# First tiles of a token-mixing and expert kernel: statistics and scans reordered, one transposed copy split in two

## The reference

```python
x0 = layernorm(x)                                 # no gain, no shift
xn1 = layernorm(x0) * g1 + b1
r, w, k, v = sigmoid(xn1 @ Wr.T), -exp(xn1 @ Ww.T), xn1 @ Wk.T, xn1 @ Wv.T
e = exp(w + k)
num[s], den[s] = decay*num[s-1] + e*v, decay*den[s-1] + e      # along the 512 tokens
tm = (r * num / (den + 1e-8)) @ Wo.T
a = x0 + tm
xn2 = layernorm(a) * g2 + b2
a = a + sigmoid(xn2 @ Wrec.T) * (square(relu(xn2 @ Wkey.T)) @ Wval.T)   # 512 hidden
x = x + a
h = layernorm(x)
x = x + shared_expert(h) + top1_of_16_experts(h)
```

## Time and profile before

| | us |
|---|---|
| median of 3 runs | 489.94 (489.55 to 490.75) |
| the profiled execution | 489.72 |
| its span | 487.7 |
| PE busy in the span | 475.4 (97%) |
| DVE busy | 370.0 (76%) |
| POOL busy | 352.1 (72%) |
| ACT busy | 323.9 (66%) |

### The profile page before, as it was taken

How to read it: one execution, slowest core, us unless ns; L and a number is a source line. 1 busy time by engine, 2 the same in 40 slices (tenths; PEclk the granted TensorE clock), 3 DMA queues, 4 the chain that set the end, 5 groups by cost and what they waited for, 6 DMA issues and landing times.

```text
span 487.7 us, 10435 instructions
## 1 busy us (share of the span) xinstructions
PE 475.4 (97%) x3079; PEld 386.6 (79%) x3079; DVE 370.0 (76%) x1056; ACT 323.9 (66%) x623; POOL 352.1 (72%) x573
## 2 busy tenths in 40 slices
PE   8998999999999999999999999999999999999995
PEld 7654777868777778686777867888899999999995
DVE  7889899899999999996899989837445555545535
ACT  2766887988978879777687886554265565555521
POOL 6665688898888988986788777777336676667760
PEclk9999999999999999999999999999999999999998
DMA  7007001101101011010101101110389755442018
GB/s 237 1 2 280 24 21 45 56 13 65 34 32 66 24 45 54 12 65 23 46 23 44 41 4 45 45 43 34 114 195 264 200 153 149 134 132 82 30 50 296
DMA packets 33031, 39.33 MB, mean 81 GB/s; under 512 B 4913, under 2 KB 29113, under 8 KB 32720
## 3 DMA queue, kind: packets, MB, share of 16 engines
q1 hardware_dynamic: 26640, 24.98, 17.7%
q0 software_dynamic: 5760, 13.16, 7.8%
q10 hardware_dynamic: 576, 0.52, 0.3%
HBM read 21.69 MB, written 17.93 MB: 81 GB/s over the span
## 4 chain that ended last, share of the span: by engine, by line
PE 83%; POOL 4%; DVE 4%; issue 4%; ACT 2%; DMA 1%; SPq 0%; POOLq 0%; DVEq 0%; ACTq 0%
PE bank L427 20%; PE bank L420 10%; PE bank L444 6%; PE bank L435 5%; PE bank L414 4%; PE bank L835 4%; PE bank L836 4%; PE bank L828 4%; PE bank L528 3%; PE bank L540 2%; PE bank L519 2%; PE bank L524 2%; PE bank L514 2%; PE bank L588 2%; PE bank L707 2%
## 5 line engine op out<-in xcount | busy, mean ns | idle before, releaser
L427 PE MATMUL bank<-hT,wm 128*128 128x256 f32 x512 | 124.7, 383 | 0.6 <-ACT kr L942 0.6
L427 PEld LDWEIGHTS bank<-hT,wm 128*128 128x128 f32 x512 | 92.0, 190 | 18.7 <-issue 8.3
L1562 POOL DMA_INDIRECT sorted_rows<-rows,posi x64 | 72.0, 1125 | 19.6 <-issue 16.9
L1646 POOL DMA_INDIRECT out<-shared x55 | 53.2, 967 | 37.3 <-DVE shared L1476 22.2
L420 PEld LDWEIGHTS bank<-wm,k 128*128 128x128 f32 x512 | 61.5, 192 | 7.3 <-issue 5.9
L420 PE MATMUL bank<-wm,k 128*128 128x128 f32 x512 | 62.2, 275 | 0.0
L1118 ACT ACTIVATE er<-bank 128x256 f32<-128x256 f32 x40 | 15.4, 384 | 44.8 <-PE bank L836 44.1
L1484 DVE TENSOR_TENSOR e<-er,bank 128x256 f32<-128x256 f32 x40 | 16.9, 421 | 23.0 <-ACT er L1118 21.1
L444 PE MATMUL bank<-wm,actA 128*128 128x128 f32 x240 | 32.9, 280 | 0.0
L1646 POOL DMA_INDIRECT out<-rows x24 | 23.1, 964 | 11.3 <-DVE rows L1476 5.3
L978 ACT ACTIVATE h<-rows,smE 128x128 f32<-128x128 f32 x64 | 26.3, 482 | 7.1 <-POOL smE L1538 7.1
(11 more groups left out here) (256 smaller groups left out, 1288.4 us busy)
## 6 DMA issues: line engine op xcount, KB each, us to landing
shared<-sorted_rows SPq DMA_DIRECT2D x56, 128.5 KB, 3.1
shared<-x SPq DMA_DIRECT2D x16, 256.0 KB
rows<-sorted_rows SPq DMA_DIRECT2D x24, 128.5 KB
wexp<-w_exp SPq DMA_DIRECT2D x2, 1536.0 KB, 8.3
sorted_rows<-filler SPq DMA_DIRECT2D x17, 128.5 KB
shared<-out SPq DMA_DIRECT2D x6, 256.0 KB, 4.9
out<-shared SPq DMA_DIRECT2D x12, 128.0 KB, 3.1
sorted_rows<-rows,posi POOLq DMA_INDIRECT x64, 2.8
```

Source lines behind the costliest of these rows:

```text
L427: ins = mm(dst[:, j * HALF:(j + 1) * HALF], W(name, 2 * pair_ + j), src[:, half * HALF:(half + 1) * HALF], start=True, stop=True)
L1562: g_.indirect_dma_start(sorted_ap, bass.IndirectOffsetOnAxis(posi[t % 3][:, g:g + 1].bitcast(U32), 0), rows[t % 3][:, g, :], None).then_in ...
L1646: g_.indirect_dma_start(out, bass.IndirectOffsetOnAxis(xr[k % RING][:, j, D:D + 1].bitcast(U32), 0), xr[k % RING][:, j, D + 1:ROW], None, ...
```

## The change

It concerns the first tiles, mostly t < 2 (`IN_HALVES`) and t < 4 (`EARLY_STATS`):

- Load of x(3) is issued ahead of the second part of the weights. DVE's start: decay constant first, statistics of x(2) and x(3) before the first round, two other constants moved into rounds (behind z of tile 0 and of tile 3).
- The scan den of tiles 1 and 2 stands in front of an of the tile before.
- For t < 2 the addition of `rstd` moves from POOL to DVE, and `xa` on POOL stands behind the power of the next tile's `smC`.
- The four products of num and q: POOL in the order 1, 3, 0, and for t < 2 the one of piece 2 on DVE. PE multiplies with Wo in the order 1, 3, 0, 2.
- T2 of tiles 0 and 1 is transposed into two banks (7 and the small bank 1), copied in halves, and the first key is formed in halves.
- T1 of tile 2 moves up in front of R of tile 1, without its warm-up of five products; ACT's copy of it and the exp of R move with it.

```diff
             load_x(2)
+            load_x(3)
             sp.dma_start(wm[:, cut:cut2], w_main[:, cut:cut2]).then_inc(s["w_in1"], 16)
-            load_x(3)
...
+        def T2_of(t, half):
+            return SMALL if t < IN_HALVES and half else T2_B
...
             def keys(t):
-                wait(pe, "xn2T", t)
+                wait(pe, "xn2T", t, 1 if t < IN_HALVES else 2)
...
+                if t < IN_HALVES:
+                    mm(KE_BANK[0][:, 0:HALF], W("Wkey", 0), xn2T[t % 2][:, 0:HALF], start=True, stop=True)
+                    wait(pe, "xn2T", t)
+                    mm(KE_BANK[0][:, HALF:T], W("Wkey", 0), xn2T[t % 2][:, HALF:T], start=True, stop=True).then_inc(s["K0"], 1)
...
                 for t in at(1):
+                    if t == 1:
+                        turn_x(t + 1)
                     if t not in (2, 3):
                         r_product(t)
...
-                        turn_x(t + 2)
-                        warm(WARM_BEFORE[1])
                         w_product(t + 2)
                         r_product(t + 2)
-                    wait(pe, "an", t)
                     wait(pe, "a", t)
-                    transposes(T2_B, an[t % 2], "T2")
+                    for half in range(2):
+                        wait(pe, "an", t, half + 1)
+                        for g in range(2 * half, 2 * half + 2):
+                            ins = nc.tensor.transpose(grp(T2_of(t, half), g), grp(an[t % 2], g), ident[:, :])
+                        ins.then_inc(s["T2"], 1)
...
             def copy_a(t):
+                if t < IN_HALVES:
+                    for half in range(2):
+                        wait(act_e, "T2", t, half + 1)
+                        af(xn2T[t % 2][:, half * HALF:(half + 1) * HALF], T2_of(t, half)[:, half * HALF:(half + 1) * HALF], ACT.Identity,
+                           bias=V("b2"), scale=V("g2")).then_inc(s["xn2T"], 1)
...
                 for t in at(4):
                     copy_a(t)
+                    if t == 0:
+                        exp_r(t + 2)
...
+            def sum_of_e(t):
+                wait(dve, "e", t)
+                wait(dve, "q", t - 2)
+                v.tensor_tensor_scan(den[t % 2][:, :], decay[:, :], e[t % 2][:, :], 0.0, ALU.mult, ALU.add).then_inc(s["den"], 1)
...
+                    if t < IN_HALVES:
+                        wait(dve, "agC", t, 2)
+                        v.tensor_scalar(smC[t % 3][:, 0, :], mvC[t % 3][:, :, 1], 1.0, LN_EPS, ALU.mult, ALU.add).then_inc(s["agC"], 1)
...
-                for t in at(0):
-                    if t == EARLY_STATS:
-                        stats_of_x(t)
+                for t in at(2):
+                    if t in (1, 2):
+                        sum_of_e(t)
                 for t in at(3):
                     norm_a(t)
...
+                    if t < 2:
+                        wait(dve, "num", t)
+                        wait(dve, "rq2", t)
+                        v.tensor_tensor(grp(q[t % 2], 2), grp(num[t % 2], 2), grp(q[t % 2], 2), ALU.mult).then_inc(s["p2"], 1)
...
                 for t in at(5):
-                    sum_a(t)
+                    if t >= 2:
+                        sum_a(t)
                 for t in at(4):
                     wait(gp, "agC", t)
-                    rstd(smC[t % 3], mvC[t % 3], "pC", t)
+                    if t < IN_HALVES:
+                        g_.tensor_tensor(smC[t % 3][:, 1, :], smC[t % 3][:, 0, :], half8[:, 0, :], ALU.pow).then_inc(s["pC"], 2)
+                    else:
+                        rstd(smC[t % 3], mvC[t % 3], "pC", t)
+                for t in at(5):
+                    if t < 2:
+                        sum_a(t)
```

More of the change, by code:

```diff
@@ L69 @@
     den=1, num=1, q=1, rq0=1, p0=1, p1=1, rq2=1, p2=1, TM2=1, p3=1, a=1,
-    agC=2, pC=2, an=1, xa=1, T2=1, xn2T=1, K0=1, kr0=1, k20=1, VAL0=1, K1=1, kr1=1, k21=1, VAL1=1, K2=1,
+    agC=3, pC=2, an=2, xa=1, T2=2, xn2T=2, K0=1, kr0=1, k20=1, VAL0=1, K1=1, kr1=1, k21=1, VAL1=1, K2=1,
     kr2=1, k22=1, VAL2=1, K3=1, kr3=1, k23=1, VAL3=1, REC=1, th=1, rv=1, x2=1, agE=2, pE=3, h=1, T4=1,
@@ L513, in keys @@
                 wait(pe, "ew", t + 1 if t else 2)
-                mm(KE_BANK[0][:, :], W("Wkey", 0), xn2T[t % 2][:, :], start=True, stop=True).then_inc(s["K0"], 1)
+                if t < IN_HALVES:
[3 more added lines that the diff above has]
+                else:
+                    mm(KE_BANK[0][:, :], W("Wkey", 0), xn2T[t % 2][:, :], start=True, stop=True).then_inc(s["K0"], 1)
                 wait(pe, "xn2T", t)
@@ L669, in one_round @@
                     if t == 1:
-                        warm(WARM_BEFORE[0])
+                        warm(WARM_BEFORE)
                     if t != 2:
@@ L713, in one_round @@
                 for t in at(2):
-                    wait(pe, "p0", t)
+                    wait(pe, "p1", t)
                     wait(pe, "xn2T", t - 1)
-                    mm(grp(TM_B, 0), grp(q[t % 2], 0), W("Wo"), start=True, stop=True)
-                    wait(pe, "p1", t)
                     mm(grp(TM_B, 1), grp(q[t % 2], 1), W("Wo"), start=True, stop=True)
@@ L720, in one_round @@
                     mm(grp(TM_B, 3), grp(q[t % 2], 3), W("Wo"), start=True, stop=True)
+                    wait(pe, "p0", t)
+                    mm(grp(TM_B, 0), grp(q[t % 2], 0), W("Wo"), start=True, stop=True)
                 for t in at(5, B_TILES):
@@ L899, in copy_a @@
             def copy_a(t):
-                wait(act_e, "T2", t)
-                af(xn2T[t % 2][:, :], T2_B[:, :], ACT.Identity, bias=V("b2"), scale=V("g2")).then_inc(s["xn2T"], 1)
+                if t < IN_HALVES:
[3 more added lines that the diff above has]
+                           bias=V("b2"), scale=V("g2")).then_inc(s["xn2T"], 1)
+                else:
+                    wait(act_e, "T2", t)
+                    af(xn2T[t % 2][:, :], T2_B[:, :], ACT.Identity, bias=V("b2"), scale=V("g2")).then_inc(s["xn2T"], 2)
             def norm_x(t):
@@ L1045, in one_round @@
                 for t in at(2):
+                    if t == 1:
+                        copy_x(t + 1)
                     if t != 2:
@@ L1146, in bn_stats_of, with bn_aggr_of @@
                 ins.then_inc(s[done], 1)
-            def bn_aggr_of(mv, st, done):
+            def bn_aggr_of(mv, st, done, count=1):
                 for g in range(G):
                     ins = v.bn_aggr(mv[:, g, :], st[:, g, :])
-                ins.then_inc(s[done], 1)
+                ins.then_inc(s[done], count)
             def normed(dst, src, mv, rs, done):
@@ L1155, in normed @@
                     ins = v.tensor_scalar(grp(dst, g), src(g), mv[:, g, 0:1], rs[:, g:g + 1], ALU.subtract, ALU.mult)
-                ins.then_inc(s[done], 1)
+                    if g % 2:
+                        ins.then_inc(s[done], 1)
             def consts():
@@ L1174, in half_tile, with decay_const, rev_const @@
                 const(ins)
-            def more_consts():
+            def decay_const():
+                dve.wait_ge(s["decay_s"], 1)
+                const(v.tensor_scalar(decay[:, :], decay[:, :], decay1[:, 0:1], None, ALU.add))
+            def rev_const():
                 for g in range(G):
@@ L1328, in one_round @@
                     v.tensor_tensor(ew[t % 2][:, :], K_B[:, :], ew[t % 2][:, :], ALU.subtract).then_inc(s["z"], 1)
+                    if t == 0:
+                        rev_const()
+                    if t == 3:
+                        place_const()
                 for t in at(6):
@@ L1360, in one_round @@
                 for t in at(2):
-                    wait(dve, "e", t)
-                    wait(dve, "q", t - 2)
-                    v.tensor_tensor_scan(den[t % 2][:, :], decay[:, :], e[t % 2][:, :], 0.0, ALU.mult, ALU.add).then_inc(s["den"], 1)
+                    if t not in (1, 2):
+                        sum_of_e(t)
                 for t in at(0):
-                    if t > EARLY_STATS:
+                    if t >= EARLY_STATS:
                         stats_of_x(t)
@@ L1408, in _ @@
             half_tile()
+            decay_const()
+            stats_of_x(2)
             consts()
-            more_consts()
-            for t in range(2, EARLY_STATS):
-                stats_of_x(t)
+            stats_of_x(3)
             def last_rounds():
```

20 lines of the change are left out of this document (9 added, 11 removed).

## The result

The changed kernel takes 496.06 us (median of 5 runs, 494.77 to 496.18) against 489.94 (5 runs, not the three named above): ratio 1.0115, 95% interval 1.0104 to 1.0126. One execution of a kernel further down (e6) took 696.52 us at a mean granted clock of 0.657 and is left out of that kernel's ratio. The forecast was 493.2, with 494.9 as the upper end: the direction holds, the size does not. The profiled execution took 496.08 (span 494.4) against 489.72 (487.7).

| event | before | after | later by |
|---|---|---|---|
| statistics of x(4) on DVE | 39.40 | 41.36 | 1.96 |
| a(2) on DVE | 50.52 | 53.72 | 3.20 |
| fourth key of tile 2 on PE | 63.62 | 68.27 | 4.65 |
| T2 of tile 4 on PE, no wait behind it in the steady part | 95.76 | 100.41 | 4.65 |
| last down product of the experts | 466.22 | 470.64 | 4.42 |

What follows compares the result with a forecast made beforehand. VectorE from 39.40 on, not TensorE, was taken to set when the steady part starts. Late loads of tiles 4 and 5 add 3.38 us: 489.72 + 3.38 = 493.1, stated as 493.2 (0.7% slower), range 491.0 to 494.9.

Steps and rivals of the forecast that it cites:

- Power, an(0), second key, a(1): Tile 0: early scan holds up GpSimd's power by 0.85 us; an(0) 0.70 later, second key and a(1) 0.40 earlier.
- The product moved to VectorE: One product behind q, up to tile 0's attention sum: might wait for GpSimd's piece of xn0, adding at most 0.44 us.
- Load of x(4): Late xa(0) delays this load's issue to 38.68; VectorE's statistics of tile 4 start at 41.25, 1.85 us later.
- From there to a(2): From tile 4's statistics through h of tile 0: the 1.85 us delay passes on unchanged, a(2) at 52.37.
- Load of x(5): Issued at 57.09 behind late xa(1); tile 5's statistics 3.55 us later, fourth key of tile 2 3.38 later.
- No hold-up: Rival, tile 0: the scan does not hold GpSimd's power; only tile 5's load costs, 1.5 to 1.7 us: 491.4. Chance 0.13.
- loads in time: Rival, statistics of tiles 4 and 5: no wait for x, head start survives: 489.0, or 487.3 without hold-up. Chance 0.15.
- TensorE's lag stays: From xa(2) on: VectorE catches up, and the 3.38 us lag carries unchanged into the total.
- the clock rival: TensorE's wait for h of tile 0 lowers its clock; up to 1.5 us more before a(2): 494.5. Chance 0.12.
- the lower bound of the hold-up: Tile 0's power beside the scan: extra 0.85 us, bounds 0 if the power starts first and 1.1, the scan's whole rest.

Runs made afterwards that it cites:

- e6: Changed kernel with GpSimd's xa of tile 1 alone back in front of the power, xa of tile 0 still behind it: 493.57 us, ratio 1.0066.
- e7: Changed kernel with xa of tiles 0 and 1 back in front of the power, product ev in the scan's place, scan behind an: 489.45 us, ratio 0.9987.
- e5: Kernel before with one edit: GpSimd's xa of tiles 0 and 1 moved behind the power of the same round: 493.29 us, ratio 1.0070.
- e1: Changed kernel with xa of tiles 0 and 1 again in front of the power, early scan kept: 489.86 us, ratio 0.9994.
- e9: e8 with GpSimd's terms of h of tile 0 (and row_ids of tile 1) ahead of its power for x(4): 490.06 us, ratio 0.9995.
- t2: Changed kernel with the load of x(3) alone put back behind the second part of the weights: 496.89 us, one run.
- e2: Changed kernel with the scan den of tiles 1 and 2 again behind an, xa still behind the power: 493.57 us, ratio 1.0067.
- e8: e7 with VectorE's statistics of x(4) moved behind the work (`mixed`) that h of tile 0 stands on: 491.99 us, ratio 1.0047.

## Why the prediction was right and wrong, step by step

- **Power, an(0), second key, a(1): right to 0.15.** The power took 1.78 (forecast 1.87: 1.02 + 0.85), starting inside the scan; an(0) at 25.01 (25.02), the second key at 27.86 (27.79), a(1) at 33.35 (33.21). The Trainium skill (SBUF — State Buffer, section "Who interferes with whom") also has a VectorE instruction with at most one input in SBUF, outside its two-port modes, not contend with GpSimd: e7's power of 1.01 beside ev agrees. The product moved to VectorE, for which I had allowed a wait of up to 0.44, took 0.29 beside xn0; no run has it alone.
- **Load of x(4): right.** Issued at 38.76 (38.68), statistics at 41.36 (41.25), +1.96 against +1.85. e5 shows the mechanism by itself.
- **From there to a(2): the first step that failed.** I let TensorE's later start pass on unchanged, +1.85, and gave a lower clock a chance of 0.12. It fell: a(2) came at +3.20. Of the gap of 1.35, 0.11 is the load and 1.23 the slower transposes and Wo products (2.81 us from T4 to a(2), before 1.58). My price for that rival was up to 1.5, and its mechanism was right, though the wait was 2.46 us and not 3.1: TensorE's work ahead of it ended later than I had it, not earlier. The 1.23 went on to T2 as priced, since xa(1) and the load of x(5) hang on a(2): issued at 58.37 where I had 57.09. The chance of 0.12 I cannot judge: in some kernels with as long a wait the clock did not fall (last section).
- **Load of x(5): size right, place wrong.** From a(2) to the fourth key I had 1.53 more (3.38 less 1.85), measured 1.45; e6, where that load is in time, takes 1.56 less from a(2) to T2. But PE waits for it at an up product of tile 0, whose bank ev of tile 3 still reads, and not at the fourth key; ev stands right behind the statistics on DVE, which I left out of the list of what they hold up.
- **No hold-up, loads in time: out.** Both powers were held; x(4) was issued after 37.
- **The last stretch: the second step that failed, and the larger one.** "TensorE's lag stays" to the end was an assumption on rows up to 100 us, put at nothing without a reason; 1.2 to 2.3 us came on behind the last expert product, with 0.3 back around the span. Its cause is open. The sum is 489.72 + 4.65 - 0.23 (up to the last expert product) + 2.28 - 0.34 = 496.08. Of the 6.36 us the terms of the forecast are 3.38, the clock 1.23, the time behind T2 1.71 net; the last 0.04 are the sizes of the two loads. e5, in whose profiled execution the late loads stand without the other two, has T2 later by 3.24, close to the 3.38.
- **The range** had the clock rival near its upper end (494.5, the range 494.9), and no room for anything behind 100 us. The clock's 1.23 alone would have stayed inside it; the last stretch took the time out.

## What to carry to other kernels

Before a step is moved back in one engine's queue, look at which transfer waits for it: here an addition of 1.3 us on GpSimd, put behind a power that still waited for VectorE, held back the next load of its buffer by 2.4 us, and the one after it by 4.4 with what had gone before (e5, counted from a(0)), and that alone made the kernel 0.7% slower, while the early scan gained 0.5 us at T2 once the buffer was freed first. Work put in an engine's gap is free only if it does not hold the engine that the gap waits for: here a product with one input in PSUM did not hold it (a power of 1.01), a scan with both in SBUF did (1.78). A wait of 2 to 3 us on TensorE may bring the clock down behind it, here at a price of 1.2 us, and that goes on to all that hangs on the result. And a change in the first tiles is to be checked at the end of the kernel too.

## What the runs showed of the hardware that I had not expected

- **The hold-up goes both ways.** an(1) started 0.05 us after POOL's xa and took 2.05 instead of 1.12; an(2) at 57.14, beside xa(1) at 57.07, took 2.06. In e1, where xa runs earlier, an(1) takes 1.11. It cost nothing here, since x(4) came later still; it only shortened VectorE's idle time ahead of the two statistics to 1.77 and 0.64 us, where I had named 2 to 3 and 1.2 to 2. The Trainium skill (SBUF — State Buffer, section "Who interferes with whom") says that `tensor_scalar` can enter a mode in which it contends with GpSimd, and that the first to issue holds the other for its whole length. The direction agrees; the size is 0.93 us, where xa had 1.20 left.
- **The earlier start does not always win.** In e9 POOL's power starts 0.07 us ahead of DVE's scan num, by the trace, and is still the one held: 2.66 us instead of 1.64, while the scan takes its 1.16. By that I should not have set the lower bound of the hold-up at 0 for a power that starts first.
- **The length of PE's wait does not tell whether the clock falls.** Behind waits of 2.46 and 2.59 us (the changed kernel twice) and 2.60 (t2) the granted clock fell to 0.50, in e9 behind 1.27; behind 2.56 (e2), 2.69 (e6) and 3.26 (e8) it stayed at 1.00. Of five runs of the changed kernel four had a mean clock of 0.993 or 0.994 and took 495.88 to 496.18, one had 0.998 and took 494.77. Of the Trainium skill's rule on idle gaps (TensorE: Matmul & The Clock Gate, section "HAM oscillation — how this bites in real kernels") these runs show the fall, but the length of the gap did not decide it.
- **The end of a kernel can change with its beginning.** No instruction of the last stretch was edited, and in the two profiled executions of the changed kernel the same loads, adds and stores took 1.2 to 2.3 us more; no run shows why.
